# First attention of a two-layer block: even chunks of context columns, four key store slots, the mask maximum moved

## What is computed

```python
scores = einsum('bsd,bmd->bsm', layernorm(x), ctx) / sqrt(256)   # ctx: (4, 1601, 256)
scores = where(mask, scores, -1e30)
readout = einsum('bsm,bmd->bsd', softmax(scores), ctx)
x = x + where(any(mask, axis=-1), readout, 0)
...
x = x + moe_0(layernorm(x))
x = x + cross_attention(layernorm(x), ctx, ...)   # k = ctx @ Wk.T + bk, v = ctx @ Wv.T + bv
x = x + moe_1(layernorm(x))
```

## Time and profile before

| | us |
|---|---|
| median of three runs (range) | 766.37 (765.65 to 770.05) |
| span of the profiled execution | 765.5 |
| PE busy | 702.9 (92%) |
| DVE busy | 537.3 (70%) |
| ACT busy | 396.4 (52%) |
| POOL busy | 174.1 (23%) |
| a batch in the steady part of the first stage | 44.8 |

### The profile page before, as it was taken

One profiled execution on the slowest core, in us unless ns is written; L12 is line 12 of the kernel. 1 busy time (PEld: TensorE's weight loads), 2 busy tenths in 40 slices (PEclk: granted clock), 3 DMA queues, 4 the chain that ended last, 5 costly groups with the idle time before them and its releaser, 6 DMA issues.

```text
span 765.5 us, 14907 instructions
## 1 busy us (share of the span) xinstructions
PE 702.9 (92%) x5499; PEld 531.4 (69%) x5499; DVE 537.3 (70%) x1174; ACT 396.4 (52%) x564; POOL 174.1 (23%) x220
## 2 busy tenths in 40 slices
PE   4899989899899999999999699999999999998990
PEld 3688878798677888888888554455455454577880
DVE  6766566657486666666667788789888878776665
ACT  2633223243322323232322599999999999533550
POOL 5461514421001000000000050002302603532551
PEclk9999999999999999999999899999999999899996
DMA  7456375642625767776778949996969840464545
GB/s 245 132 172 232 122 263 175 221 166 87 186 78 195 248 209 235 253 234 206 237 253 136 192 74 142 209 136 102 210 109 186 128 71 2 133 268 126 166 127 191
DMA packets 55212, 131.16 MB, mean 171 GB/s; under 512 B 12160, under 2 KB 29952, under 8 KB 51568
## 3 DMA queue, kind: packets, MB, share of 16 engines
q1 hardware_dynamic: 51888, 122.93, 60.5%
q0 software_dynamic: 2256, 6.18, 2.4%
q10 hardware_dynamic: 1008, 1.25, 0.5%
HBM read 78.78 MB, written 48.79 MB: 167 GB/s over the span
## 4 chain that ended last, share of the span: by engine, by line
PE 55%; ACT 12%; issue 11%; DVE 9%; DMA 7%; POOL 4%; SPq 1%; DVEq 0%; POOLq 0%; ACTq 0%
PE ps L656 12%; PE ps L657 12%; PE ps L658 12%; ACT p L1438 8%; PE ps L1000 5%; PE ps L958 4%; PE ps L1188 4%; DMA raw<-in_ctxT 2%; PE ps L1204 2%; POOL cTl L612 2%; DMA raw<-in_ctxN 2%; DMA k_lo<-kl 1%; PE ps L1022 1%; ACT cNh L1267 1%; POOL cNl L599 1%
## 5 line engine op out<-in xcount | busy, mean ns | idle before, releaser
L1438 ACT ACTIVATE p<-ps,kbias 128x1024 f32<-128x1024 f32 (+1 forms) x208 | 211.3, 1163 | 5.2 <-PE ps L958 5.0
L1946 DVE TENSOR_SCALAR p<-p 128x1024 f32<-128x1024 f32 (+1 forms) x208 | 140.9, 689 | 26.1 <-ACT p L1438 24.5
L1000 PE MATMUL ps<-p,vsl 128*17 128x256 f32 (+1 forms) x1664 | 113.9, 383 | 2.0 <-DVE p L1946 1.0
L1343 ACT ACTIVATE hh<-h 128x512 fp32r<-128x512 f32 x50 | 31.6, 632 | 132.9 <-DVE h L1813 115.9
L958 PEld LDWEIGHTS ps<-qst,kst 48*128 48x128 f32 (+1 forms) x832 | 58.6, 182 | 60.2 <-ACT p L1438 32.7
L958 PE MATMUL ps<-qst,kst 48*128 48x256 f32 (+1 forms) x832 | 91.1, 318 | 5.5 <-ACT p L1438 1.5
L359 POOL TENSOR_SCALAR nv<-mv 128x2 f32<-128x2 f32 x8 | 6.2, 774 | 359.6 <-DVE mv L1876 211.8
L656 PE MATMUL ps<-xTh,w_hi 128*128 128x512 f32 x200 | 79.8, 399 | 1.5 <-DVE h L1809 0.8
L657 PE MATMUL ps<-xTl,w_hi 128*128 128x512 f32 x200 | 79.2, 396 | 0.0
L658 PE MATMUL ps<-xTh,w_lo 128*128 128x512 f32 x200 | 78.9, 394 | 0.0
L1000 PEld LDWEIGHTS ps<-p,vsl 128*17 128x17 f32 (+1 forms) x1664 | 35.9, 96 | 39.6 <-issue 7.1
(11 more groups left out here) (308 smaller groups left out, 1551.3 us busy)
## 6 DMA issues: line engine op xcount, KB each, us to landing
x_slots<-blank SPq DMA_DIRECT2D x20, 1032.0 KB, 5.9
kst<-k_hi SPq DMA_DIRECT2D x64, 200.2 KB, 9.1
w_raw<-in_w SPq DMA_DIRECT2D x25, 384.0 KB, 3.5
v_one<-vst SPq DMA_DIRECT2D x4, 1768.0 KB, 8.9
vsl<-v_one SPq DMA_DIRECT2D x4, 1768.0 KB, 17.4
kst<-k_lo SPq DMA_DIRECT2D x32, 200.2 KB, 8.8
raw<-in_ctxN SPq DMA_DIRECT2D x12, 512.0 KB, 5.7
k_hi<-kh SPq DMA_DIRECT2D x24, 256.0 KB, 2.6
```

The costliest lines, as they stand in the source:

```text
L1000: mm = pe.matmul(ps[32 * j:32 * j + VW, 6 + job % 2, 0:SEQ], vsl[0:rows, b % 2, at_:at_ + VW], p32[0:rows, x % PBUF, (2 * t + c) * SEQ:(2 ...
L1343: act.activation(hh[:, half, :], h32[:, half, :], ACT.Copy).then_inc(hh_rdy, 1)
L1438: act.activation(p32[0:rows, x % PBUF, :], psf[0:rows, bank * 512:bank * 512 + 1024], ACT.Exp, scale=0.25, bias=kbias[0:rows, col:col + 1] ...
L1946: dve.tensor_scalar(t, t, CLO, CHI, ALU.max, ALU.min).then_inc(p_clip, 1)
```

## The change

The 1602 columns are cut into 400, 400, 400 and 402. There are four slots for keys instead of three, each 402 columns wide instead of 512; since a half has four units, a slot now always serves the same chunk. `masks` keeps only `neg`. The maximum becomes `any_key(b)`, done in the first row tile of the batch, behind the row maxima, the first two `klo` and `add_readout` of the tile before, and ahead of `row_scale`. One semaphore, `rsum_rdy`, is merged into `rscale_rdy`. Numbers of instructions are the same.

```diff
--- before.py
+++ after.py
@@ -30,7 +30,8 @@
 MW = -(-M // 4)
 MT = -(-M // P)
 TAIL = M - (MT - 1) * P
-MCH = [(c * 512, min(512, MP - c * 512)) for c in range(-(-MP // 512))]
+MCW = MP // 4 // 2 * 2
+MCH = [(c * MCW, MCW if c < 3 else MP - 3 * MCW) for c in range(4)]
 NH, HD = 16, 16
 NG = 4
 HG = NH // NG
@@ -50,7 +51,7 @@
 TPC = [(0, 0, 1024), (1, 0, 1024), (0, 1024, MP - 1024), (1, 1024, MP - 1024)]
 NI = 2 * NB
 NK = 2 * len(MCH)
-KSLOT = 3
+KSLOT = 4
 NJ = NB * NG
 NALL = NJ * MT
 KR = 3 * HD
@@ -128,7 +129,7 @@
             rsum = A("rsum", [P, 1])
             rscale = A("rscale", [P, 1])
             pTh, pTl = A("pTh", [P, MT, P], F32R), A("pTl", [P, MT, P], F32R)
-            kh, kl = A("kh", [P, KSLOT, 512], F32R), A("kl", [P, KSLOT, 512], F32R)
+            kh, kl = A("kh", [P, KSLOT, MCH[3][1]], F32R), A("kl", [P, KSLOT, MCH[3][1]], F32R)
             vst = A("vst", [P, MT, NH, VW])
 
         with ExitStack() as s:
@@ -279,7 +280,7 @@
         cT_rdy, cT_ev, dl_rdy, dl_ev, dl_st, dl_mv, dl_g, dl_r, beta_rdy = (sem(n) for n in ("cT_rdy", "cT_ev", "dl_rdy", "dl_ev", "dl_st", "dl_mv", "dl_g", "dl_r", "beta_rdy"))
         rg_rdy, nw, rs_rdy, lg_ev = (sem(n) for n in ("rg_rdy", "nw", "rs_rdy", "lg_ev"))
         out_done, out_go = sem("out_done"), sem("out_go")
-        rsum_rdy, rscale_rdy = sem("rsum_rdy"), sem("rscale_rdy")
+        rscale_rdy = sem("rscale_rdy")
         wraw_free = sem("wraw_free")
         x_zero, d_cst, tri_rdy = sem("x_zero"), sem("d_cst"), sem("tri_rdy")
         d_in = [sem(f"d_in{n}") for n in range(2)]
@@ -1563,7 +1564,12 @@
 
                 dve.wait_ge(att_in, b * 16 + 16)
                 dve.tensor_scalar(neg[:], attend, 1.0, 1.6e31, ALU.subtract, ALU.mult).then_inc(neg_rdy, 1)
+                dve.wait_ge(neg_rdy, b + 1)
+
+            def any_key(b):
+
                 dve.tensor_reduce(valid[:], attend, AX.X, ALU.max).then_inc(att_free, 1)
+                dve.wait_ge(att_free, b + 1)
 
             def klo(b, n):
                 mt, (c0, w) = n // 4, MCH[n % 4]
@@ -1609,14 +1615,14 @@
             def add_readout(i):
 
                 dve.wait_ge(R_rdy, i + 1)
-                dve.wait_ge(rscale_rdy, i + 1)
+                dve.wait_ge(rscale_rdy, 2 * i + 2)
                 dve.scalar_tensor_tensor(out=resid[:, i, :], in0=ps[:, PVB, 0:D], scalar=rscale[:], in1=resid[:, i, :], op0=ALU.mult, op1=ALU.add).then_inc(R_ev, 1)
 
             def row_scale(i):
 
                 dve.wait_ge(exp_rdy, i + 1)
-                dve.reciprocal(rsum[:], psum_[:]).then_inc(rsum_rdy, 1)
-                dve.wait_ge(rsum_rdy, i + 1)
+                dve.reciprocal(rsum[:], psum_[:]).then_inc(rscale_rdy, 1)
+                dve.wait_ge(rscale_rdy, 2 * i + 1)
                 dve.tensor_tensor(rscale[:], rsum[:], valid[:], ALU.mult).then_inc(rscale_rdy, 1)
 
             def next_stat(t0, t1):
@@ -1650,8 +1656,6 @@
                 dve.tensor_tensor(cTl[:, 0, k, 0:1024], raw[:, k, :], cTh[:, 0, k, 0:1024].bitcast(F32), ALU.subtract).then_inc(ctx_split, 1)
             norm_lo(0)
             masks(0)
-            dve.wait_ge(neg_rdy, 1)
-            dve.wait_ge(att_free, 1)
             for i in range(NI):
                 b, h = i // 2, 4 * (i % 2)
                 last = i == NI - 1
@@ -1665,6 +1669,8 @@
                 klo(b, h + 1)
                 if i:
                     add_readout(i - 1)
+                if h == 0:
+                    any_key(b)
                 row_scale(i)
                 if last:
                     next_stat(3, NT - 2)
@@ -1692,8 +1698,6 @@
                     norm_lo(b + 1)
                 if h and b + 1 < NB:
                     masks(b + 1)
-                    dve.wait_ge(neg_rdy, b + 2)
-                    dve.wait_ge(att_free, b + 2)
             next_stat(NT - 2, NT - 1)
             for q, bank in enumerate((SB0, SB0 + 1, TB0)):
                 next_lo(q, bank)
```

## The result

| | before | after |
|---|---|---|
| median of seven runs, us (range) | 766.37 (763.36 to 770.05) | 760.52 (759.39 to 762.05) |
| span of the profiled execution, us | 765.5 | 759.1 |
| first attention, from the first scores to the work behind it, us | 186.2 | 181.7 |

The ratio of after to before is 0.9924 with a 95% interval of 0.9904 to 0.9944: 5.8 us faster, where 10.9 were forecast, and 0.5 us above the top of the range. Of the 6.4 us between the two profiled executions, 4.4 lie ahead of the end of the first attention.

What follows compares the result with a forecast made beforehand. TensorE's stream was taken as the bound, plus a handful of waits. Batches 1 and 2 gave -7.3 us, batch 0 -1.2, batch 3 -2.4: -10.9 in total, so 755.5 us, range 752.8 to 760.0.

Steps and rivals of the forecast that it cites:

- the wait of 0.65: TensorE's third transpose group in a batch's first half, waiting for `ptl` behind the moved `valid`: +0.65 us, bounds 0 and 1.8.
- +0.2 at the end: First tile of batch 0, bound by VectorE: `valid` returns behind two `klo`, partly falling into gaps, costing 0.2 us.
- three signs of being wrong: Second-half wait of 1.5 us or more; TensorE waiting for `cTl` at a batch's start; changed length behind the first attention.
- Price of a column: TensorE's matmuls of 400 columns take 0.181 us, between 256 and 512; a score tile 4.36 us, 0.40 less.
- rival 2: Only columns count on TensorE, so the even cut saves nothing there; 762.4 us, chance 0.06.
- rival 4: A TensorE matmul of 400 columns is paced like one of 512, 0.230 us; 774.5 us, chance 0.02.
- Maximum out of the scores' way: First half of batches 1 and 2: without `valid` ahead, TensorE's third-bank wait goes; scores 6.17 to 4.36 us, -1.81.
- Rival 3: VectorE hides the moved maximum because the transposes come later than counted; 753.5 us, chance 0.10.
- The second half: Second score tile of batches 1 and 2: 0.6 us wait at the third chunk, scores 4.96 us, -0.48.
- rival 1: Fuller key stores delay the context load on which the next rows' split depends; 758.3 us, chance 0.18.
- Slots: Four key slots end ScalarE's 2.32 us wait for a key store; TensorE gains 1.1 us in batches 1 and 2.
- rival 5: The fourth slot does nothing, as something else held ScalarE's key copy; 758.2 us, chance 0.04.

Runs made afterwards that it cites:

- Experiments 2: The changed kernel with `rscale` formed by an instruction with one tensor input and `valid` as scalar operand, same place; 752.95 us, 0.9827 of the kernel before.
- experiment 9: The changed kernel with only GpSimd's first `cNl` of a batch waiting until `rscale` is done; 752.96 us, 0.9815 of the kernel before.
- experiment 1: The changed kernel with the mask maximum straight behind the row maxima, ahead of the first `klo`; 751.14 us, 0.9809 of the kernel before.
- experiments 3: The changed kernel with the mask maximum back in `masks`, so new chunks and four slots alone; 758.22 us, 0.9894 of the kernel before.
- experiment 5: The kernel before with only the chunks of columns changed, three slots and the maximum in its old place; 765.60 us, ratio 1.0009.

## Why the prediction was wrong

The step that failed is "`valid` 71.45 to 73.3, two small scalings to 73.7, `ptl` to 74.4". The second scaling took 2.00 us, so that the wait of 0.65 became 2.06 in batches 1 to 3, above the bound of 1.8 that I had set. In batch 0, where "+0.2 at the end" was put for `valid`, it became 2.92; there 1.9 are `valid` itself, a term too small, and the rest is the collision. In their place before, both scalings ended 1.3 us ahead of POOL's first `cNl` (71.64 + 0.16 and 73.11, above); at 73.3 to 73.7 they lay in it. I moved three instructions on DVE's timeline and looked for who waits for them, but not at what runs beside them in the new place. Experiments 2 and 9 show the cause by two ways that share nothing but the collision; 9 leaves DVE's program as it is.

What the four batches gave, from first scores to first scores (batch 3: to the work behind the stage), in us:

| batch | forecast | after | experiment 9 |
|---|---|---|---|
| 0 | -1.20 | -0.73 | -1.63 |
| 1 | -3.66 | -2.41 | -3.96 |
| 2 | -3.66 | -1.75 | -4.02 |
| 3 | -2.40 | +0.39 | -1.29 |
| sum | -10.9 | -4.50 | -10.90 |

The two measured columns differ by 6.4 us: about what the collision cost in this stage. With it out, the sum is the forecast one. That it meets to a tenth is luck: batch 3 fell short by 1.1, batches 0, 1 and 2 gave the same more. And batch 3 holds a stretch at the lower clock that no term foresaw; experiment 1, without it, gave -3.50 there. The stretches from 180 to 188 us, experiment 1 and then 9:

```profile
180.00:188.00 8.00, 6.12 (x53) 5.97 (x51) 4.21 (x12) 1.27 (x3) 0.00 (x0) 0.99 0.23 57
180.00:188.00 8.00, 7.31 (x52) 7.17 (x50) 3.36 (x9) 1.36 (x4) 0.00 (x0) 0.83 0.03 3
```

Timed, experiment 9 gains 13.6 us, 2.7 beyond its stage's share; why the part behind the stage is shorter too stays open. A change of that part was one of the three signs of being wrong, and the only one that came; experiments 3 and 5, which leave the maximum in its old place, show it too, so it has nothing to do with the step that failed.

By its other steps:
- **Price of a column**: forecast 0.181 and 4.36 for a tile; 0.18, and 4.40 (164.91 to 169.31) to 4.50, so 0.26 to 0.36 less than 4.76 where 0.40 was put. Right; the rule that only columns count (rival 2) and the dear 400 (rival 4) fall with it. The price of rival 2 has a slip: 16 x (0.40 + 0.46) counts the stream twice, there being eight row tiles; 8 x 0.86 is the 6.9 that 762.4 goes by. The prediction also has the notes say more than they do. The Trainium skill, page TensorE: Matmul & The Clock Gate, section Back-to-back issue gap, gives its formula for a single matmul by itself, and says that it counts too little for few columns in a stream of weight loads and matmuls. This kernel is such a stream, so the formula was no case against the edit.
- **Maximum out of the scores' way**: the wait at the third chunk is gone in every even tile. Right; 6.17 became 4.48, by 0.12 less than forecast.
- **What `valid` itself costs in its new place**: forecast 0.65, measured 0.21 to 0.28 in batches 1 to 3 of experiments 2 and 9. A size, on the safe side. Rival 3 (it hides wholly) is nearly true there without the collision, but not in batch 0 (1.88 and 1.95).
- **The second half**: a wait of 0.6 forecast at its third chunk, 0.78 measured in batch 1, none in batch 2, which PE reached later. The tile of batch 1 took 5.49 us, not 4.96, and so gave nothing (5.44 before). The late load (rival 1) is real, but a bound only once PE is early: 1.38 in experiment 1.
- **Slots**: forecast -1.1 a batch; the waits are gone, and the end of a batch from the last readout on is 7.18 us instead of 8.45. Right in the sum, and rival 5 falls. But the chunks' gain hangs on it, which the sum with its separate terms doesn't say: without it they are worth nothing (experiment 5).
- **The clock** was in no step. The stretch at the lower level in batch 2 comes behind the collision's wait and is in none of experiments 1, 2 and 9, which have no such wait: a part of the same mistake, 1.45 us. The one near the end of batch 3 is not: experiments 2 and 9 have it too. It comes behind a wait of 1.81 us for `vst`, and experiment 1 has the same wait without it. What decides stays open.

## What to carry over

An instruction that is moved takes its inputs' ports with it: before moving it, read what GpSimd runs at the new time, not only who waits for the result, and try a form with one tensor input for a small product (for 128x1 it was enough; not every such form goes free, as the rows below show). When a large change gives half of what was summed, look for an instruction whose duration changed though its shape did not; one grouped view of durations before and after shows it. Edits that each remove one of several waits in a row are to be costed together.

## What the runs showed of the hardware

- A 128x1 product with two SBUF inputs took 0.16 us alone, up to 2.00 us beside a GpSimd subtraction; the form with `valid` as a scalar operand 0.21 to 0.22 beside the same one.
- One tensor input alone does not free an instruction. In the kernel before, the first `xn` of batch 0, 128x256 with one tensor input, took 1.38 us and ended 0.14 us behind GpSimd's subtraction; the five after it took 0.40 each. In experiment 9 the first took 1.98 (30.90 to 32.88; GpSimd until 32.73). DVE and POOL of the kernel before:

```profile
31.36 1.38 DVE L1554 TENSOR_SCALAR xn<-resid,mv,rstd 128x256 f32<-128x256 f32 x1
```

```profile
27.85 4.75 POOL L599 TENSOR_TENSOR cNl<-raw,cNh 128x1024 fp32r<-128x1024 f32 x2 [6.00 <-ACT cNh L1267]
```

- It goes the other way too: a GpSimd subtraction of 128x578 took 2.26 us instead of 1.21 with DVE's 0.98 us `neg` inside it.
- Three waits of 2.06 us at the same place of three batches had different ends: two were followed by a granted clock of 1.00, one by 0.64. What decides was not tried.
